# Graph attention, four layers, 16 graphs: the next graph's layer-0 tiles run between layer 2 and layer 3

## What is computed

```
x = _layernorm(x + _L0_gnn_ref(x, adj, L0_gnn_W, L0_gnn_a), axis=-1)
x = _layernorm(x + _L1_gnn_ref(x, adj, L1_gnn_W, L1_gnn_a, L1_gnn_bias), axis=-1)
x = _layernorm(x + _L2_gnn_ref(x, adj, ...), axis=-1)
x = _layernorm(x + _L3_gnn_ref(x, adj, L3_gnn_lin_w, L3_gnn_lin_b, L3_gnn_W_w, L3_gnn_a), axis=-1)

# layers 0 and 1 (layer 1 adds a bias, with slope 0.1)
e = leaky_relu(s_src[:, :, None] + s_dst[:, None, :], 0.2)
attn = softmax(where(adj > 0, e, NEG_BIG), axis=-1)
elu(einsum('bij,bjf->bif', attn, h))
# layer 2: eight heads, scores q k^T plus a bias per edge type
# layer 3: e = sum over f of a[f] * leaky_relu(u[i, f] + v[j, f]), then softmax and attn @ hp
```

## Time and profile before

| | us |
|---|---|
| median of 3 runs | 8829.6 (8818.0 to 8830.2) |
| span of the profiled execution | 8820.9 |
| one graph's layer 2 (start at 2392.6) | 196.5 |
| the passage behind it, from the last score to the ring's first group | 42.9 |
| the ring behind that | 298.7 |
| the last graph's ring, with nothing of a next graph in it | 240.8 |
| before the first layer 2 starts | 263.8 |

### The profile page before, as it was taken

The page is one execution under the profiler, slowest core; times in us unless marked ns, Lnnn a source line. Parts: engine busy times, 40 slices in busy tenths (PEclk is TensorE's granted clock), DMA queues, the critical chain, the costliest instruction groups (busy, mean ns, idle before and its releaser), DMA issues.

```text
span 8820.9 us, 165559 instructions
## 1 busy us (share of the span) xinstructions
PE 7888.1 (89%) x57857; PEld 3520.0 (40%) x58440; DVE 7363.6 (83%) x11117; ACT 7107.8 (81%) x8295; POOL 1432.9 (16%) x582
## 2 busy tenths in 40 slices
PE   3898998989989899898989989899898998989999
PEld 2434435344353433434334343343534435344342
DVE  3788887988879888798888988888788887988888
ACT  2788787977879788797887978879797786977878
POOL 0301204021040310303012030120402104021000
PEclk7999999999999999999999999999999999999999
DMA  2614426144261532516235171442614426153250
GB/s 69 166 37 104 114 54 160 42 120 96 58 151 49 136 75 72 139 49 156 50 90 127 45 175 34 102 116 56 160 40 115 103 53 155 47 129 82 61 126 19
DMA packets 430043, 822.72 MB, mean 93 GB/s; under 512 B 163874, under 2 KB 221218, under 8 KB 427042
## 3 DMA queue, kind: packets, MB, share of 16 engines
q1 hardware_dynamic: 429090, 810.76, 38.1%
...
## 4 chain that ended last, share of the span: by engine, by line
PE 31%; issue 27%; SPq 18%; ACT 16%; DVE 5%; POOL 2%; DMA 1%; ACTq 0%; DVEq 0%; POOLq 0%
PE psum L881 18%; SPq L437 18%; ACT work L1108 11%; PE psum L663 2%; ACT spare L950 2%; PE psum L585 2%; ACT spare L945 2%; PE psum L580 1%; PE psum L758 1%; PE psum L599 1%; DVE work L1331 1%; PE psum L848 1%; DVE work L1492 1%; PE psum L733 1%; PE psum L771 1%
## 5 line engine op out<-in xcount | busy, mean ns | idle before, releaser
L881 PE MATMUL psum<-work,pick 128*32 128x512 f32 x32768 | 3750.9, 598 | 116.9 <-ACT work L1108 58.3
L1108 ACT ACTIVATE work<-spare,ucol 128x1024 f32<-128x1024 f32 x3477 | 3702.4, 1142 | 13.3 <-PE psum L881 10.1
L1492 DVE TENSOR_SCALAR work<-spare,ucol 128x1024 f32<-128x1024 f32 x4715 | 3204.2, 745 | 72.1 <-PE psum L881 53.8
L881 PEld LDWEIGHTS psum<-work,pick 128*32 128x32 f32 x32768 | 979.7, 110 | 2439.1 <-issue 2059.4
L1018 ACT ACTIVATE work<-psum,beta 128x1024 f32<-128x1024 f32 x1024 | 1140.0, 1113 | 549.8 <-PE psum L733 397.6
L1359 DVE STREAM_TRANSPOSE work<-work 128x1024 f32<-128x1024 f32 x960 | 1191.0, 1241 | 263.7 <-DMA work<-work 203.0
L1331 DVE CUSTOM_DVE_ANT_0 work<-psum,work 128x1024 f32<-128x1024 f32 x1024 | 1225.2, 1197 | 176.8 <-ACT work L1018 168.3
L1025 ACT ACTIVATE work<-work,least 128x1024 f32<-128x1024 f32 x1024 | 1173.0, 1145 | 19.6 <-DVE least L1331 19.6
L1575 POOL TENSOR_TENSOR rstd<-rstd,neg_half 128x8 f32<-128x8 f32 x64 | 131.7, 2057 | 5198.1 <-DVE rstd L1269 5198.1
L733 PE MATMUL psum<-x_split,q_hi 128*128 128x512 f32 x2048 | 860.3, 502 | 0.0
L729 PE MATMUL psum<-mask,ident_b 128*128 128x512 bf16 x1793 | 587.6, 399 | 299.8 <-DVE least L1331 272.3
...
## 6 DMA issues: line engine op xcount, KB each, us to landing
...
adj_in<-in_adj SPq DMA_DIRECT2D x128, 512.0 KB, 5.1
q_lo<-adj_in SPq DMA_DIRECT2D x1024, 64.0 KB, 2.0
q_lo<-spare SPq DMA_DIRECT2D x1024, 64.0 KB, 2.0
...
```

What stands on the lines that cost most here:

```text
L881: mm = pe.matmul(slot[32 * q:32 * q + 32, cols], pick[:, 15 - kk:47 - kk], ring[kk % 4][q][:, cols], start=False, stop=(kk == 15), skip_gr ...
L1108: ins = act.activation(ring[kk % 4][q], v3, ACT.Relu, bias=ucol[:, 4 * T + q, kk:kk + 1])
L1492: ins = dve.tensor_scalar(ring[kk % 4][q], v3, ucol[:, 4 * T + q, kk:kk + 1], 0.0, ALU.add, ALU.max)
```

## The change

The eight tiles of the next graph's layer 0 leave the ring. They now lie in the passage, between the last products of layer 2, and use layer 2's two score areas and its four buffers `probs` in turn. Their column and values are made in `turn` during layer 2 (steps 27 and 29). The transposed pairs get two destination buffers, so that one can be moved while the other is read. In the ring, PE multiplies pairs 2 and 3 at u = 2 and 5, layer 0 ends from u = 7, and layer 1 runs one tile in seven groups from u = 27, ending from u = 91. The last instructions of the work ahead are at u = 114 instead of 127. The last four tiles of layer 2 (`exps`, `turn_tile`, `pv_last`, `turn_heads`) move from `layer2` behind the loop's end into `layer3`. The `KEEP` matmuls are gone. Layer 3's values are made behind group 0 instead of ahead of the ring, and the last graph but one has its own copy of the loop's body.

```diff
-SPAN = 63
+PAIRS_0 = {2: 2, 5: 3}
+END_0, TILE_1, GAP_1, PAIR_1, END_1 = 7, 27, 7, 47, 91
...
+    if pair + 1 == HP:
+        return {3: ("next_column", 0), 5: ("next_values", 0)}.get(t)
...
-        pairA_T = q_lo[:, 1, :, :].rearrange("p a b -> p (a b)").bitcast(F32)
+        pairA_T = [q_lo[:, i, :, :].rearrange("p a b -> p (a b)").bitcast(F32) for i in range(2)]
```

SP's `layer3`:

```diff
             def layer3(g):
-                move_pair(g + 1, 0)
-                move_pair(g + 1, 1)
-                move_tile(g, 0)
...
+                for m in range(NT // 2):
+                    move_pair(g + 1, m)
+                for u in range(GROUPS):
+                    T, kk = divmod(u, 16)
+                    if T and kk == 6:
+                        move_tile(g, T - 1)
+                    m = tile_1(u, 5)
+                    if m and m % 2:
+                        move_pair(g + 1, m // 2)
```

PE's `layer3`:

```diff
             def layer3(g, it, more):
-                pe.wait_ge(s_leaky, g * TILES2 + TILES2)
-                if more:
-                    first_products(g + 1)
-                for i in range(KEEP):
-                    pe.matmul(outT[:, 0:HALF], ident_b[:], mask[:, 0, 0:HALF], start=True, stop=True)
+                tile_0(0)
+                pv_quad(g, it, MOVED - 2, 0, None)
+                tile_0(1)
+                turn_tile(g, it, TILES2 - 2)
+                pv_quad(g, it, MOVED - 2, 1, None)
+                tile_0(2)
+                turn_tile(g, it, TILES2 - 1)
+                pv_last(it, 0)
+                tile_0(3)
+                pv_quad(g, it, MOVED - 1, 0, None)
+                tile_0(4)
+                pv_quad(g, it, MOVED - 1, 1, None)
+                tile_0(5)
+                pv_last(it, 1)
+                turn_heads(g, it, HP - 1)
+                tile_0(6)
                 if more:
+                    pv_pair(g + 1, 0)
+                tile_0(7)
+                if more:
+                    pv_pair(g + 1, 1)
                 both_ready(ONE + it[1] + it[0][("xT2", 0)], s_xn2, g * 2 + 2)
...
+                    if u == 0:
...
+                        make_values(score[1], xTa[:], linT_s[:, :]).then_inc(s_side, 1)
```

ACT's:

```diff
             def layer3(g, it, more):
+                exps(g, TILES2 - 2)
+                relu_of(0)
+                exps(g, TILES2 - 1)
+                relu_of(1)
+                exp_of(0)
+                copy_out(g, HP - 1, 0)
+                relu_of(2)
...
+                    if u == 1:
+                        act.wait_ge(s_side, g * 2 + 2)
+                        act.activation(values[3], score[1].rearrange("p (j c) -> p j c", c=P)[:, :, 0:F], ACT.Copy)\
+                           .then_inc(s_side_act, 1)
```

DVE's:

```diff
             def layer3(g, it, more):
+                leaky_of(0)
+                turn_tile(g, it, TILES2 - 2)
+                leaky_of(1)
+                blocks_of(0)
+                turn_tile(g, it, TILES2 - 1)
+                leaky_of(2)
+                blocks_of(1)
...
+                blocks_of(4)
+                dve.wait_ge(s_probs, g * TILES2 + TILES2)
                 link(dve.reciprocal(rinv[:], rowsum[:, (HP - 1) % 2, :]))
```

More of the change, by code:

```diff
@@ L439, in move_quads @@
             def move_quads(g, more, tail):
[L440 removed]
+                for each in s_moved_a:
+                    ready(each, (g * (NT // 2) + NT // 2) * MOVE_DONE)
                 if more:
@@ L938, in relu_a, with relu_0 @@
+            def relu_0(g, m, values_in, it):
                 if m == 0:
-                    act.wait_ge(s_values0_read, g + 1)
-                elif t == 0:
+                    in_sbuf(act, *values_in)
+                if m >= 4:
+                    act.wait_ge(s_blocks_a, g * 2 * NT + m - 3)
+                elif it is not None:
+                    filled(act, before(it) if m < 2 else it, ("tile", TILES2 - 4 + m))
+                act.wait_ge(s_scores_0, g * NT + m + 1)
+                act.activation(probs[m % 4], score[m % 2], ACT.Relu, bias=sbias[:, m:m + 1], scale=GAIN[0])\
+                   .then_inc(s_relu_a, 1)
```

543 lines of the change are left out of this document (302 added, 241 removed).

## The result

The changed kernel takes **9053.98 us** (median of 4 runs, 9048.0 to 9065.9) against 8826.39 us of the kernel before on the same chip: a ratio of 1.0268, with a 95% interval of 1.0255 to 1.028. It was predicted as slower, at 8900 us in a range up to 8990. The sign was right and the size wrong by 154 us.

What follows compares the result with a forecast made beforehand. PE was taken to bound the ring. Passage +10, ring -1.7 and layer 2 -1.5 us over 15 graphs give +102, the start -32: 8820.9 + 70 = 8891, plus 8.7 for the median, 8900 us; range 8740 to 8990.

Steps and rivals of the forecast that it cites:

- What leaves the ring: PE's work in the ring falls 11.0 us: scores 9.0 and two pairs 3.9 leave, layer 3's value product 1.9 enters.
- The new waits: In the ring, units or row moves reach PE late at three places, together 9.3 us.
- (a): Group 1 of the ring: PE waits 2.8 us for two ACT units behind the copy of layer 3's values.
- (b): Ring, u = 10 to 15: layer 0's end with its long DVE work now comes early, about 1.5 us.
- (c): Ring, u = 47: PE waits for pair 4's row move, with the next score behind it, 5 us in all.
- the waits do not come: Rival: less loaded ACT and DVE are early enough at all three ring places; ring sheds 11.0 us, whole 8708; chance 0.18.
- the ring sheds ACT's and DVE's 20 us: Rival: ACT and DVE bound the ring, which sheds 20 us; whole 8573 us; chance 0.04.
- The passage: From layer 2's last score to the ring: loop's turn, row moves and half clock add 10 us (6.8 to 14).
- slower still: Rival: half clock through the passage's tail; passage +14 us, ring -0.5, whole 8978; chance 0.14.
- The Trainium skill's rule: Rival: initiating a DMA takes little time, so row moves are no load; passage 43 us, whole 8750; chance 0.02.
- Layer 2: Layer 2 shortens by 1.5 us: DVE's jump starts earlier (-2.2), the values on PE add 0.7.
- Once: Ahead of the first layer 2, SP's 10.4 us sets the pace: layer 0 gains 17, layer 1 15, together -32 us.

Runs made afterwards that it cites:

- b_nokeep: The kernel before without its 16 KEEP matmuls on nothing: 8849.9 us, ratio 1.0034.
- e_clk: Changed kernel with layer 0's four pairs multiplied in the ring, tile 4's blocks behind the normalisation, 32 matmuls on nothing ahead of turned x2: 8907.1 us.
- e_best: Changed kernel with e_clk's edits, layer 3's values made and copied ahead of the ring, layer 1's pairs multiplied at groups 58 to 79: 8714.5 us.
- e_pair50: Changed kernel with layer 1's pairs multiplied three groups later, behind the next score (groups 50 to 71): 9030.9 us, ratio 1.0252.
- e_pairs: Changed kernel with layer 0's pairs 0 and 1 also multiplied in the ring and layer 1 eight groups later: 9035.4 us, ratio 1.0251.

## Why the prediction was right and wrong

**What leaves the ring.** A ring's length less PE's idle time, and less half of the half clock in which PE works (3.0 us before, 10.1 of the 11.3 after), is its work at full clock. That gives 298.4 - 10.6 - 1.5 = 286.3 before and 281.0 after, a fall of 5.3 us. But the 10.6 are not all idle time. The trace of before lacks 19 matmul records a ring, 14 of them at L643, and each leaves a gap of 0.16 us that looks like a wait:

```profile
2668.74 1.92 PE L881 MATMUL psum<-work,pick 128*32 128x512 f32 x16
2670.60 0.60 PE L643 MATMUL psum<-mask_next,ident_b 128*128 128x512 bf16 x2
...
2671.60 1.93 PE L881 MATMUL psum<-work,pick 128*32 128x512 f32 x16
...
2681.65 0.38 PE L643 MATMUL psum<-mask_next,ident_b 128*128 128x512 bf16 x1 [0.16 <-issue]
```

The score with both records takes 2.86 us from group to group (2668.74 to 2671.60), and so does the one of the earlier trace rows, which has one record and the gap. b_nokeep has the same instructions in its ring and all 19 records: 7.7 us idle, 289.1 of work. Without the false gaps before has 7.8 us idle and 289.1 of work as well. So the work fell by 8.1 us, where I had 11.0. The price of a score holds. 1.2 us of the difference are the second query's matmuls: they stood behind the ring's last group before (L627) and are in the ring now, which I had overlooked. For the other 1.7 us no row gives a reason.

**The new waits: the term that failed most in the ring.** I had 9.3 us. PE's idle time grew from 7.8 to 17.8 and the half clock in which it works by 7.1, worth 3.5: 13.5 us. By place, idle time and half clock under work in us a graph, with the time from the ring's start (the false gaps of before are left out):

| | 0 to 15 | 15 to 110 | 110 to 150 | 150 to 250 | rest |
|---|---|---|---|---|---|
| before | 0.0, 3.0 | 2.0, 0 | 1.5, 0 | 1.8, 0 | 2.5, 0 |
| after | 2.8, 6.5 | 4.4, 2.1 | 4.2, 1.2 | 4.7, 0.2 | 1.8, 0 |

(a) Group 1: 2.76 us of wait for 2.8 predicted, and 3.5 us more of half clock that I had not set down, 1.8 us. In the last graph, where I had written 0, passage and ring together grew from 283.1 to 287.3.
(b) Layer 0's end: the waits are there (0.62 and 2.25 us at 2748.4 and 2754.6 in graph 4). In this stretch 2.4 us of idle time are new, and the clock takes 1.0 more, where I had 1.5 in all:

```profile
2748.42 3.91 PE L928 MATMUL psum<-work,pick 128*32 128x512 f32 x32 [0.62 <-ACT work L1205]
2754.58 5.71 PE L928 MATMUL psum<-work,pick 128*32 128x512 f32 x36 [2.25 <-DVE work L1625]
```

(c) Pair 4: right in place, 2.46 us and the product behind it at half clock (3.17 for 1.95), 3.3 us by the table where I had 5:

```profile
2835.87 3.17 PE L697 MATMUL psum<-q_lo,vw 128*64 128x256 f32 x16 [2.46 <-DMA q_lo<-adj_in]
```

(d) Between 150 and 250 us stand 3.0 us more, for which I had put nothing. The largest of them is a wait for a move of layer 3's own, which PE never had in the ring before and now has in 14 of the 16 (total, times, longest):

```profile
PE psum L862 <- DMA work<-work: 24.7, 14, 2.1
```

In graph 4 SP issued pair 5 from 2851.88 to 2862.72 and this tile directly behind it, from 2863.00; PE got it at 2875.70. I had looked for what stands ahead of pair 4 on SP's queue and not for what stands behind pair 5.

The whole ring: 10.0 + 3.5 - 8.1 = 5.4 for the 5.5 measured. Its error of 7.2 us is 2.9 of work and 4.2 of waits. The two rivals in which the waits do not come, or the ring sheds ACT's and DVE's 20 us, fell with the first of these numbers.

**The passage: mechanism right, clock and loop's turn too small.** The walk along the queues put pair 0's move at 17.0 us, pair 1's landing at 39.0 and x2 at 38; graph 4 has 19.6, 41.7 and 40.5. The 2.7 us are in its first products: the loop's turn gave half clock for the score and one product (3.68 us instead of 1.95). Behind pair 1 the excess over full clock is 1.7 + 0.9 + 1.0 + 1.8 + 0.4 = 5.8 us, from the rows above. I had 4.2 for both places and subtracted nearly half, since KEEP's slow time was in the old passage. For the passage, the case called "slower still", half clock through its tail at +14, is the one that came; its 8978 for the whole was too low as well.

The experiments do not split the 12.6 us by cause. Taking both waits away, with the two products, gave 5.4 us, and filling the idle time 5.1 more (e_clk); that leaves 2.1 above before, but before had 13.9 us of half clock of its own. What the tiles themselves cost shows in two other passages. By the code, graphs 0 and 14 carry the eight tiles and have no turn of the loop in their passages. There DVE's first transpose for pair 0 begins 8.0 to 8.1 us behind the last score, in after and in the other runs, against 11.0 to 14.7 us in graphs 1 to 13 of after. Their passages take 48.1 and 51.3 us in after, where graphs 1 to 13 have a mean of 56.3, and 41.0 and 41.2 in e_best, where these have 48.0. In the kernel before, graph 0 has the one passage with work of a next graph and without a turn: 40.4 us, 11.4 of them at half clock. So in e_best, which has none of that in graph 0, the eight tiles cost less than 1 us on balance, and the loop's turn, with the clock behind it, costs 7. In after it is 5 to 8, where I had 2.8 and 1.9 for the clock. The tiles did find room, as the windows had promised; what did not is the turn, and no run moved it.

The Trainium skill's rule (DMA: Bandwidth & Descriptors, Issuing engines are not separate DMA queues) that starting a DMA costs little against the DMA would have made the passage 43 us; the trace does not agree with it. Pair 1's sixteen DMAs were issued over 10.42 us and had landed 1.4 us later; the passage was 55.9.

**Layer 2** gained 3.8 us where 1.5 was predicted. DVE's jump went behind the ring's end as foreseen. The rest goes with the clock: half clock in layer 2 fell from 19.5 to 12.1 us. Over all runs the length of layer 2 (192.4 to 198.2) goes up with that time: 10.5 to 13.3 us in the runs below 194.5, 14.1 to 19.5 in those above. That is a correlation; no run changed layer 2 alone.

**Once: the step "now SP's 10.4 is the pace" failed for layer 1.** For layer 0 it held: moves at 76.6, 86.7, 96.9 and 107.5, and the last landed 11 us earlier than before, not 17, since the first came later, not earlier. For layer 1 it was wrong in sign. I had taken the two buffers for a licence to overlap and had not looked at PE's queue, where `pv_pair(4)` (u = 47) stands ahead of the score of tile 11 (u = 48). With that order, two buffers are no better than one, and the pace rose from 15.4 to 21.5 us. e_pair50 gives the 29 us back.

**Sum.** Ring +7.2 and passage +2.6 against their terms, layer 2 -2.3: 15 x 7.5 = 112, and 39 for the start: 151 of the 154 us. So the steps that failed are the ring's new waits (9.3 for 13.5), its work (11.0 for 8.1), the passage's clock and turn, and the pace of the first graph's layer 1. The range was too narrow since every bound of a wait was its own length without the clock behind it, the waits behind pair 5 were put at nothing, the work term had no bound of its own, and the start's sign was never doubted.

## What to carry to other kernels

Price a new wait on PE as its length and the half clock behind it: at the ring's start 1.8 us on a wait of 2.8. Where two waits end together, removing one shows little; remove both before calling either harmless. If some graphs pass a place without the loop's turn, compare them with the others before blaming the work there. Before calling idle time idle, count the matmul records against the code. Before trusting that a second buffer overlaps anything, read where the consumer's queue has the product and where the next tile's score. A change that looks 2.7% worse can be 1.2% better once the order of a few instructions is mended.

## What the runs showed of the chip

- Half clock went on under full work. Windows of after, from the wait for pair 1 on, as above:

```profile
2693.10:2703.30 10.20, 5.53 (x24) 2.96 (x24) 5.09 (x10) 0.28 (x1) 2.03 (x1) 0.50 0.41 100
2706.70:2716.90 10.20, 10.20 (x25) 2.23 (x23) 7.08 (x10) 2.91 (x4) 0.00 (x0) 0.50 0.37 91
```

  In the second PE is busy for all of 10.2 us and has 0.50. Thirty-two small matmuls of 0.22 us each in the idle time took 19 us of half clock out of the passage (e_clk).
- The price of half clock depends on the place: 10 us of it cost the passage of after 3.5 us (graphs 4, 5, 12 against 6, 8, 13), 19 us 5.1 (e_clk, by its profile), where ACT's and DVE's steps lie between the products; b_nokeep had 10.7 us more of it and lost 1.5 there.
- Taking work off PE (e_pairs: two products of 1.95 us) came with more half clock in the passage, 25.7 us instead of 19.7, and the passage fell by 1.7 us only.
- At the loop's turn PE stood 2.81 us before and stands 3.62 now (DVE's copy is named as what ended it); with the half clock behind, the passage without it is 5 to 8 us shorter in after and 7 in e_best.
